# The six transformer layers as straight code on all five engines, with every wait on a constant

## What is computed

```python
for i in range(DEPTH):          # DEPTH = 6
    x = attn_layer(shift_tokens(x), Wqkv[i], q_scale[i], k_scale[i], Wo[i]) + x
    x = ffn_layer(shift_tokens(x), ln_g[i], ln_b[i], W1[i], b1[i], W2[i], b2[i]) + x

def attn_layer(x, Wqkv, qs, ksc, Wo):      # 16 heads of 64, windows of 32 keys
    q, k, v = heads(x @ Wqkv)
    q, k = rotary(l2norm(q) * qs), rotary(l2norm(k) * ksc)
    return local_attention(q, k, v) @ Wo   # own window and the one before, softmax

def ffn_layer(x, g, bln, W1, b1, W2, b2):  # hidden size 341
    a, gate = split((layernorm(x) * g + bln) @ W1 + b1)
    return a * gelu(gate) @ W2 + b2
```

## Time and profile before

| | |
|---|---|
| time before, median of 3 runs | 5275.22 us (5266.4 to 5277.52) |
| the profiled execution | 5285.3 us, its span 5283.6 us |
| PE busy | 4847.9 us (92%) |
| DVE, ACT, POOL busy | 3947.9, 3873.8, 2399.3 us |
| the windowed transformer | from about 1300 us to the end of the span |
| a layer of it | about 655 us |
| mean granted TensorE clock | 0.949 |

### The profile page before, as it was taken

How to read it: one execution, slowest core, us unless ns; L and a number is a source line. 1 busy time by engine, 2 the same in 40 slices (tenths; PEclk the granted TensorE clock), 3 DMA queues, 4 the chain that set the end, 5 groups by cost and what they waited for, 6 DMA issues and landing times.

```text
span 5283.6 us, 143381 instructions
## 1 busy us (share of the span) xinstructions
PE 4847.9 (92%) x42260; PEld 4066.3 (77%) x42260; DVE 3947.9 (75%) x10954; ACT 3873.8 (73%) x12542; POOL 2399.3 (45%) x3729
## 2 busy tenths in 40 slices
PE   7989689992799988999899998999989999799996
PEld 4668679882688877888678886888868888688885
DVE  6666757776688867888678886788858888588886
ACT  2334433434799968999689996899959999599995
POOL 0000000001566636666366663666636666366660
PEclk8989879995899999999999999999989999899998
DMA  1002000001111111111111111111111111111110
GB/s 38 2 1 57 23 1 0 0 0 45 27 25 28 28 46 31 28 25 28 48 30 28 28 28 49 28 28 25 28 50 28 28 28 25 50 30 26 28 28 25
DMA packets 105574, 144.70 MB, mean 27 GB/s; under 512 B 65485, under 2 KB 77026, under 8 KB 104610
## 3 DMA queue, kind: packets, MB, share of 16 engines
q1 hardware_dynamic: 97826, 111.01, 9.0%
q0 software_dynamic: 7040, 25.13, 1.5%
HBM read 44.87 MB, written 2.10 MB: 9 GB/s over the span
## 4 chain that ended last, share of the span: by engine, by line
PE 64%; DVE 3%; issue 3%; ACT 3%; POOL 1%; DMA 1%; SPq 0%; DVEq 0%; ACTq 0%; POOLq 0%
PE d_S_ps L1948 12%; PE d_O_ps L1972 9%; PE d_PT_ps L1981 7%; PE d_A_ps L1905 7%; PE d_T_ps L1912 7%; PE d_PT_ps L1958 6%; PE d_A_ps L1907 5%; PE d_A_ps L1906 5%; PE d_S_ps L1945 2%; DMA d_xs<-d_xb 1%; PE d_A_ps L2099 1%; PE d_S_ps L2084 1%; PE d_O_ps L2099 1%; POOL d_qk L1768 1%; DVE d_ff_stats L2449 1%
## 5 line engine op out<-in xcount | busy, mean ns | idle before, releaser
L2170 ACT ACTIVATE d_probs<-d_S_ps,d_neg_max 128x96 f32<-128x96 f32 x3072 | 1000.8, 342 | 13.4 <-DVE d_neg_max L2392 3.8
L1768 POOL TENSOR_TENSOR d_qk<-d_qk,d_sin_terms 128x512 f32<-128x512 f32 x768 | 961.5, 1273 | 32.7 <-DVE d_sin_terms L2364 32.7
L1948 PEld LDWEIGHTS d_S_ps<-d_kT,d_q_blocks 128*128 128x128 f32 x6144 | 791.2, 192 | 2.3
L1948 PE MATMUL d_S_ps<-d_kT,d_q_blocks 128*128 128x96 f32 x6144 | 790.4, 272 | 0.0
L2364 DVE TENSOR_TENSOR d_qk<-d_A_ps,d_tables 128x512 f32<-128x512 f32 x768 | 527.0, 686 | 216.0 <-ACT d_squares L2126 149.1
L2170 ACT ACTIVATION_READ_ACCUMULATOR d_probs<-d_S_ps,d_neg_max 128x1 f32 x3072 | 639.4, 208 | 0.0
L1905 PE MATMUL d_A_ps<-d_wqkv_hi,d_xT_hi 128*128 128x512 f32 x1152 | 557.0, 484 | 23.3 <-DVE d_sin_terms L2364 16.9
L2126 ACT ACTIVATE d_squares<-d_A_ps 128x512 f32<-128x512 f32 x768 | 462.8, 603 | 126.3 <-PE d_A_ps L1907 126.1
L2364 DVE TENSOR_TENSOR d_sin_terms<-d_A_ps,d_tables 128x512 f32<-128x512 f32 x768 | 522.0, 680 | 0.0
L2178 ACT ACTIVATE d_probsT<-d_PT_ps 96x512 f32<-96x512 f32 (+1 forms) x768 | 460.2, 599 | 79.3 <-PE d_PT_ps L1958 79.2
L1912 PE MATMUL d_T_ps<-d_ident,d_qk 128*128 128x128 f32 x3072 | 484.6, 281 | 34.0 <-POOL d_qk L1805 30.2
(11 more groups left out here) (422 smaller groups left out, 10729.7 us busy)
## 6 DMA issues: line engine op xcount, KB each, us to landing
d_v_early<-d_v SPq DMA_DIRECT2D x192, 256.0 KB, 3.0
d_v_early<-d_v SPq DMA_DIRECT2D x192, 128.0 KB, 2.3
d_tables<-L_ffn_rotary POOLq DMA_DIRECT2D x5, 2048.0 KB, 8.3
d_qk<-L_ffn_Wqkv POOLq DMA_DIRECT2D x15, 512.0 KB, 3.9
d_xs<-d_xb SPq DMA_DIRECT2D x56, 127.0 KB
d_xs<-d_xb SPq DMA_DIRECT2D x96, 63.5 KB
ax_fp_blocks<-L_ffn_blocks_gu SPq DMA_DIRECT2D x16, 256.0 KB, 3.6
ax_fp_scales<-L_ffn_scales_gu SPq DMA_DIRECT2D x64, 64.0 KB, 2.9
```

The lines of the kernel that those rows point to most:

```text
L1768: nc.gpsimd.tensor_tensor(c4[:, :, s, :], c4[:, :, s, :], s4[:, :, 1 - s, :], ALU.add).then_inc(rotated, 1)
L1948: last = nc.tensor.matmul(S[g % 2][:, n * SEEN:(n + 1) * SEEN], qx[:, p, half, :], kT[b][jj][:, p, HALF * half:HALF * half + SEEN], start= ...
L2170: nc.scalar.activation(pr[:, g, n, seen_columns(g)], S[g % 2][:, n * SEEN:(n + 1) * SEEN], ACT.Exp, bias=nmax[:, g, n:n + 1], accum_out=de ...
```

## The change

Each `Fori` over the layers becomes a loop of Python, so that the six layers stand one behind the other in each engine's stream. `l` is then a number, every wait compares with a constant, and the register instructions and branches of the layer loop are gone. All `sem_inc(waits_met)` of this part are taken out. No operation, tile, buffer or order of work is changed. The register loops of the other blocks stay.

```diff
                 def early_values(l, u, b, jj):
                     sp.wait_ge(v_copied, l * VALUES_IN_LAYER + (u * 2 + 2))
-                    sp.sem_inc(waits_met)
                     sp.wait_ge(pv_ps, l * (4 * U) + (u * 4 + 3))
-                    sp.sem_inc(waits_met)
...
-                with sp.Fori(0, DEPTH) as l:
+                for l in range(DEPTH):
...
                     def shift_group(g):
                         sp.wait_ge(resid_f, (l * GROUPS + g) * 2 + 6)
-                        sp.sem_inc(waits_met)
                         sp.wait_ge(shift_main, DMA * (l * SHIFTS + (GROUPS + J) + g))
-                        sp.sem_inc(waits_met)
                         shift(g * 2, 2, shift_main)
...
                     pool.wait_ge(k_newton, n * K_STEPS + 2)
-                    pool.sem_inc(waits_met)
                     nc.gpsimd.tensor_scalar(k_work[:, 0, :], k_work[:, 1, :], -10.0 / 3.0, None, ALU.add).then_inc(k_newton, 1)
...
-                with pool.Fori(0, DEPTH - 1) as l:
+                for l in range(DEPTH - 1):
                     layer(l)
                     next_weights(l)
                 layer(DEPTH - 1)
...
-                with pe.Fori(0, DEPTH) as l:
+                for l in range(DEPTH):
...
-                with act.Fori(0, DEPTH) as l:
+                for l in range(DEPTH):
...
-                with v.Fori(0, DEPTH) as l:
+                for l in range(DEPTH):
```

More of the change, by code:

```diff
@@ L2216, in group_guess @@
                         act.wait_ge(f_ve, ms * 2 + 2)
-                        act.sem_inc(waits_met)
                         rsqrt_guess(nc, fve[:], frt[:], guess_offset[:, 0:1]).then_inc(f_guess, 1)
@@ L2453, in group_variance @@
                         v.wait_ge(f_stat, ms * 4 + 4)
-                        v.sem_inc(waits_met)
                         for t in range(G4):
```

## The result

The changed kernel takes 5236.66 us in the median of four runs (5234.03 to 5238.76), the kernel before 5272.6 us in four runs of its own (5266.4 to 5277.52). The ratio is 0.993, with a 95% interval from 0.9918 to 0.9943: 36 us less, where 30 were forecast. It is faster by more than the 0.2% that a measurement can tell, and 5236.66 lies inside the stated range.

What follows compares the result with a forecast made beforehand. PE was taken to bound the kernel, setting the tiles' pace. Savings of 21.4 + 2.0 + 3.6 + 2 + 1 = 30.0 us, off the median of 5275.22, gave 5245 us, range 5229 to 5262.

Steps and rivals of the forecast that it cites:

- The edges on PE: Between layers: PE's idle holes shrink to 1.06 us each as register instructions and branch go; 21.4 us saved.
- What I said of ACT and DVE: At layer edges: their branches run while PE idles anyway, and removed they make nothing next to be late; no size.
- The key norm: Prologue, POOL: each removed `sem_inc` saves 0.12 us on what PE waits for; 3.6 us over five layers.
- The clock: Behind each edge: shorter idleness may hold PE's clock through the first projection; 0.4 us per edge, 2 us.
- The sign that I gave: Six microseconds behind the edge: PE's clock over 0.50 if the clock term is right.
- The entry into the feed-forward part: PE's first load behind DVE's end: fewer register instructions and waits, 0.34 us in each of six layers, 2.0 us.
- rival 4: Feed-forward start: engines collide otherwise, 2 us a layer either way, 5235 or 5255 us; 5%.
- The tail: SP's row copies at the end: less waiting and counting between issues, some five groups at 0.2 us, 1 us.
- The tiles: Attention tiles: PE's back-to-back matmuls cover its register instructions, so removing them gains 0 and the period stays 17.15 us.
- rival 1: Attention tiles: register instructions do hold PE, so 111 us more are saved, about 5134 us; 4%.
- Rivals 2 and 3: Code fetching: hole moved, not removed, 5263 us, 7%; or longer streams run short of code, slower, 5306 us, 4%.
- The sum: Whole kernel: all terms together save 30.0 us.

Runs made afterwards that it cites:

- e8: Kernel before with the layer loops of ACT, DVE, POOL and SP straight, PE's loop three rounds of two layers, all `sem_inc`s kept: 5257.83 us.
- e2: Kernel before with only PE's layer loop made straight code, the other four loops and all `sem_inc`s kept: 5271.06 us, ratio 0.9991.
- e9: Changed kernel with three `sem_inc`s put back in the norm of the keys on POOL: 5242.48 us.
- e3: Kernel before with the layer loops of ACT, DVE, POOL and SP straight, PE's loop and all `sem_inc`s kept: 5270.21 us, ratio 0.9993.
- e1: Kernel before with all five layer loops made straight code, every `sem_inc` kept: 5242.32 us, ratio 0.9934.
- e4: Changed kernel with two waits ahead of the next tile's transpose exchanged, so the wait for ACT's copy sits on the matmul: 5226.0 us, ratio 0.9896.

## Why the prediction was right, step by step

- *The edges on PE*, 21.4 forecast, 21.5 measured. The idle time left is 1.04 for 1.06, and in e8 only the edges with a branch keep their hole. What I said of ACT and DVE was right for this change alone. As a statement on the branches it hid that DVE's is the next late thing: with PE's loop alone gone, PE waits for DVE's split, and e2 gains nothing that the measurement tells.
- *The key norm*, 3.6 forecast, 3.2 by the length of the norms and 3.6 by the start of the attention in e9. My 0.12 compared two different steps; for one and the same it is 0.11. All `sem_inc`s are 4.6.
- *The clock*, 2 forecast with 4.3 as bound: this is the mis-sized term, since the prologue gave 12.1 us and 4.6 of these are the counting. The 7.5 left are beyond my bound, and how much of them is the clock isn't known. The sign that I gave, a clock over 0.50, came true, but it tells little: in the six microseconds from the first transpose the five edges have 0.65, 0.62, 0.50, 0.51 and 0.63 before and 0.65, 1.00, 0.64, 0.70 and 0.66 after. Most of the 7.5 us come with PE's loop: between e3 and e1, which differ in nothing else, the attention starts 1.24 us earlier per edge (33.37 and 32.13), 6.2 us in five. Of the 1.24 us, 0.47 are there at the first rotation (6.34 and 5.87 us behind the first transpose): the first projection matmul took 0.76 to 0.77 us behind each long hole of before and takes 0.47 at every edge of the changed kernel's first profile. The rest comes later in the prologue, which I had left out. One part of it is seen: in two of five edges of the first profile of before, one of five in the second and one in e3, attention started some 1.9 us later than in the mean of the others, and there PE's clock fell to half once more behind its wait for POOL. In the changed kernel that wait is shorter and none of ten edges shows it. That PE's missing register instructions have a share in the 6.2 isn't excluded; no run separates the two.
- *The entry into the feed-forward part*, 2.0 forecast. In the first two profiles the hand-over is shorter by 0.42 us in five layers and by 0.33 in one, 2.4 in all. It doesn't show as such in the sum, as the stretch behind it varies by more (rival 4): with it −7.3 us, of which two profiles each can't say how much is the change's.
- *The tail*, 1 forecast: 0.1. The groups still come every 9.13 us; it seems that SP's waits and counting lay beside the transfers that follow each other, but no run tests this.
- *The tiles*, 0 forecast: the removed register instructions gave nothing, so rival 1 is out. My reason, PE's matmuls back to back, was wrong at one place. In the changed kernel the period was also set by ACT's copy and its hand-over, which e4 shows.
- *Rivals 2 and 3*: the holes were removed, not moved. The instruction queues moved less than before (q8 316 packets for 338).
- *The sum*, 30 for 36. That it came so near is in part luck: the edges are right by mechanism, but the prologue gave some 6 us more than its two terms, the tiles 2.5 the other way, and the feed-forward stretch can't be told from chance.

## What to carry to other kernels

A loop whose body is long pays its branch on every engine that the next body's first chain needs, so it has to go on all of these at once; here one engine at a time was worth nothing that the medians tell. Where an instruction has two waits, the one that is fulfilled last belongs on the instruction itself, even where the profile shows no idle time ahead of it. Before a term of a few microseconds is read from two profiles, take each kernel's profile twice: here stretches that no change touched differed by 8 us.

## What was not expected of the hardware

The same code ran its tiles with a period whose median was the same within 0.01 us in all layers of an execution and different between executions (17.146 and 17.16 before, 17.18 and 17.167 after). And the branch of PE costs 208 ns in a short loop and 3.6 us in a long one, while DVE's record of its branch has 63 ns and the 2.5 us come behind it, as idle time without a releaser.
